# The end of a mixture of experts: the sums of two tables are added on GpSimd before VectorE adds them to the residual

## What is computed

```python
x = x + L0_attn(layernorm(x))
x = x + L0_xattn(layernorm(x), ctx_2048, mask)
x = x + L0_ffn(layernorm(x))        # group attention, then a mixture of experts
x = x + L1_attn(layernorm(x))
x = x + L1_xattn(layernorm(x), ctx_2048, mask)
x = x + L1_ffn(layernorm(x))
```

```python
moe = jnp.einsum('tei,te,eih->th', act, wfull, Wd)
shared = jax.nn.silu(t @ Wsg) * (t @ Wsu) @ Wsd
return resid + (moe + shared).reshape(B, S, H)
```

## Time and profile before

| | |
|---|---|
| median of 3 runs | 2375.61 us (2370.52 to 2378.47) |
| the profiled execution, its own time | 2365.98 us |
| its span, first to last instruction | 2364.2 us |
| mean granted TensorE clock | 0.96 |
| busy: PE, DVE, POOL, ACT | 92%, 55%, 42%, 39% |

### The profile page before, as it was taken

The page is one execution under the profiler, slowest core; times in us unless marked ns, Lnnn a source line. Parts: engine busy times, 40 slices in busy tenths (PEclk is TensorE's granted clock), DMA queues, the critical chain, the costliest instruction groups (busy, mean ns, idle before and its releaser), DMA issues. The chain is left out here.

```text
span 2364.2 us, 40797 instructions
## 1 busy us (share of the span) xinstructions
PE 2163.3 (92%) x14955; PEld 1575.4 (67%) x14955; DVE 1311.1 (55%) x2409; ACT 927.3 (39%) x1667; POOL 987.0 (42%) x852
## 2 busy tenths in 40 slices
PE   7889999798999998879999999697889999989998
PEld 7658877577888887633333333286667777759997
DVE  4563677647787878543333333585862666653333
ACT  1332322335454543236666665214632332322221
POOL 2333565456656564306666665353533110002220
PEclk9899999799999999989999999898999999979999
DMA  3011100221111210466666888620021001001110
GB/s 127 34 50 54 41 28 2 76 67 55 58 54 54 67 45 23 169 231 165 141 144 143 224 219 275 185 81 35 3 77 44 27 27 41 1 27 54 54 53 32
DMA packets 56926, 194.38 MB, mean 82 GB/s; under 512 B 8244, under 2 KB 8500, under 8 KB 49844
## 3 DMA queue, kind: packets, MB, share of 16 engines
q1 hardware_dynamic: 36676, 147.45, 18.0%
q0 software_dynamic: 17280, 38.94, 8.4%
q10 hardware_dynamic: 2784, 5.51, 0.6%
HBM read 158.71 MB, written 33.16 MB: 81 GB/s over the span
## 5 line engine op out<-in xcount | busy, mean ns | idle before, releaser
L2260 PE MATMUL bank<-m_ring,m_bT 128*64 x576 | 266.6, 606 | 3.7 <-ACT m_upper L1988 3.4
L2262 PE MATMUL bank<-m_upper,m_bT 128*64 128x512 f32 x576 | 266.7, 606 | 0.0
L2183 DVE SCALAR_TENSOR_TENSOR m_prod<-bank,m_slot_rows,m_silu 64x256 f32<-64x256 f32 x144 | 69.6, 483 | 276.0 <-ACT m_silu L1934 273.4
L2260 PEld LDWEIGHTS bank<-m_ring,m_bT 128*64 128x64 f32 x576 | 73.9, 138 | 142.6 <-issue 142.6
L1906 POOL DMA_INDIRECT m_sum<-m_yb,m_idx x72 | 102.8, 1428 | 130.3 <-DVE m_yb L2194 111.2
L970 ACT ACTIVATE y_att_p_rows<-bank,y_att_n_top 112x375 f32<-112x375 f32 x128 | 71.6, 572 | 188.6 <-DVE y_att_n_top L1012 188.6
L1988 ACT ACTIVATE m_upper<-m_ring 128x1024 f32 x144 | 143.5, 1046 | 2.5 <-issue 2.4
L2288 PE MATMUL bank<-m_ring,m_aT 128*64 x288 | 135.4, 592 | 0.7 <-DVE m_aT L2200 0.7
L2290 PE MATMUL bank<-m_upper,m_aT 128*64 128x512 f32 x288 | 135.4, 592 | 0.0
L313 PE MATMUL bank<-f_hT_hi,f_w_hi 128*128 128x448 f32 x288 | 113.4, 394 | 13.6 <-POOL f_w_lo L1436 3.2
L2474 POOL TENSOR_TENSOR z_w_lo<-z_raw,z_w_hi 128x1024 fp32r<-128x1024 f32 x21 | 50.6, 2408 | 155.4 <-ACT z_w_hi L2500 155.4
(11 more groups left out here) (477 smaller groups left out, 6208.5 us busy)
## 6 DMA issues: line engine op xcount, KB each, us to landing
m_ring<-in_m_w SPq DMA_DIRECT2D x32, 1536.0 KB, 8.2
f_raw<-in_f_wq SPq DMA_DIRECT2D x64, 256.0 KB, 2.6
z_raw<-in_z_w SPq DMA_DIRECT2D x7, 1536.0 KB, 6.7
f_att_wo_raw<-in_f_wo SPq DMA_DIRECT2D x16, 512.0 KB, 4.1
m_sum<-m_slot_rows SPq DMA_DIRECT2D x4, 2048.0 KB, 18.0
x_c_raw<-in_ctxT SPq DMA_DIRECT2D x8, 752.0 KB, 8.9
y_c_raw<-in_ctxT SPq DMA_DIRECT2D x8, 752.0 KB, 9.7
a_raw<-in_a_wqk SPq DMA_DIRECT2D x8, 256.0 KB, 2.5
```

Of the source, the lines that this page charges most:

```text
L2260: pe.matmul(ps_gu[u % 2][0:HP, :], bT[:, n % 2, k, 0:HP], ring[:, bass.ds(slot + at, D)], start=(k == 0), stop=(k == KC - 1))
L2262: o = pe.matmul(ps_gu[u % 2][HP:P, :], bT[:, n % 2, k, HP:P], upper[:, n % 2, at:at + D], start=(k == 0), stop=(k == KC - 1))
```

## The change

GpSimd gets seven adds behind its last scatter: for each tile it waits for both loads of the pair of tiles and adds `x2` to `y` in place. VectorE loses its seven first adds. It adds `y`, which then holds both tables' sums, to `x`, once per tile, when GpSimd's `first_sum` says that the tile is there. Both shared tiles are now added ahead of all of these.

```diff
@@ GpSimd, behind the last scatter
             scatter(NBLK - 1)
+            for b in range(NT):
+                pool.wait_ge(early_in[b // 2], 16)
+                pool.wait_ge(late_in[b // 2], 16)
+                pool.tensor_tensor(y[:, b, :], y[:, b, :], x2[:, b, :], ALU.add).then_inc(first_sum, 1)
@@ VectorE
-            def add_first(b):
+            def add_sums(b):
                 dve.wait_ge(add_done, b + 1)
-                dve.wait_ge(early_in[b // 2], 16)
-                dve.tensor_tensor(x[:, b, :], x[:, b, :], y[:, b, :], ALU.add).then_inc(first_sum, 1)
-
-            def add_last(b):
-                dve.wait_ge(late_in[b // 2], 16)
                 dve.wait_ge(first_sum, b + 1)
-                dve.tensor_tensor(x[:, b, :], x[:, b, :], x2[:, b, :], ALU.add).then_inc(total_sum, 1)
+                dve.tensor_tensor(x[:, b, :], x[:, b, :], y[:, b, :], ALU.add).then_inc(total_sum, 1)
                 dve.wait_ge(total_sum, b + 1)
                 dve.bn_stats(g.stats[:, b, :], x[:, b, :])
@@ VectorE, the order at the end
             add_shared(5)
-            for b in range(6):
-                add_first(b)
             add_shared(6)
-            add_first(6)
             for b in range(NT):
-                add_last(b)
+                add_sums(b)
```

## The result

The changed kernel takes 2380.74 us in the median of 20 runs (2373.21 to 2388.83), the kernel before 2371.24 us over 20 runs (2364.00 to 2378.47). The ratio is 1.0042, with a 95% interval of 1.0031 to 1.0053. That is 7.4 to 12.6 us slower, where +2.9 us was forecast.

A forecast was written before the change was run, and what follows sets the result against it. VectorE's chain was taken to bound the mixture's end; with GpSimd's adds and turns of 1.69 us it would end at 1535.5 instead of 1532.55, +2.9 us, put on the median 2375.61: 2378.5 us, range 2371 to 2386.

The forecast's parts named there:

- VectorE's chain and not TensorE sets the end of the stage: At the mixture's end, VectorE's seven pairs of add and statistics, ending at 1532.55, were said to hold up the next stage.
- The turns: In the final adds, GpSimd and VectorE, both reading SBUF, were to alternate, five turns of 1.69 us each.
- VectorE's own end: End of VectorE's last statistics in the mixture, forecast at 1535.5 instead of 1532.5, +2.9 us.
- The lower bound: At the mixture's end, without disturbance between the engines, VectorE would finish at 1532.05 to 1532.1, -0.45 us.
- The rival without disturbance: In the final adds, the engines would not hold each other up: -0.45 us, 2375.2 us in all; chance 10%.
- the one in which GpSimd keeps its place until all its adds are done: VectorE's seven pairs would start only after GpSimd's seven adds, at 1530.6: +7.4 us, 2383.0 us; chance 5%.
- Nothing is queued behind these seven adds on GpSimd but the barrier: At the mixture's end, GpSimd's queue was taken to hold only the barrier after its adds, with no further time counted.
- what moves the 1532.55 moves everything behind the barrier by as much: At the mixture's end, any shift of VectorE's end was to shift the barrier and next stage equally.
- it is a mixture that ends 2.9 us later: By the trace, the mixture's end was to come 2.9 us later; chance of this forecast 75%.
- The clock: TensorE's return to full clock, some 3 us after resuming, was to move in step; rival: later, +1.5 us, chance 10%.
- three signs of being wrong: At the mixture's end: GpSimd adds all 1.27 us, VectorE's first add ending after 1530, or x2 loads landing outside 1522 to 1525.

The follow-up runs named there:

- e6: Kernel before, with VectorE adding shared tile 6 ahead of the y adds of tiles 4 and 5: 21.79 us from last scatter to next stage, ratio 0.9989.
- e10: Kernel before, with e6's order and the last adds of tiles 1 to 3 on TensorE: 21.25 us from last scatter to next stage, ratio 0.9997.
- e3: Changed kernel, with VectorE's seven final adds reading a PSUM bank in place of y: 29.58 us from last scatter to next stage, ratio not measured.
- e8: Changed kernel, with a GpSimd drain behind its last scatter and VectorE's final adds reading PSUM: 22.96 us from scatter to next stage, ratio 1.0003.
- e4: Changed kernel without GpSimd's drain at the end of the mixture's block: 25.71 us from last scatter to next stage, ratio 1.0016.
- e2: Kernel before, with GpSimd waiting for VectorE's last add, then setting one unused element: 31.73 us from last scatter to next stage, ratio 1.0043.

## Why the prediction's number held, and where its mechanism failed

What was right: in the kernel before, VectorE's chain and not TensorE sets the end of the stage (in e6 and e10 the chain ends 1.21 and 1.75 us earlier after the scatter, and the next stage begins as much earlier). The turns: 1.69 us forecast for one, 1.67 us measured from one VectorE add to the next (1528.02 to 1529.69 in the trace); first add 1.7 forecast and 1.66 measured, the others 1.0 to 1.1 and 1.03. What GpSimd waits out of VectorE's add is 1.71 - 1.26 = 0.45 of 0.675 us. The Trainium skill, "SBUF — State Buffer", section "Who interferes with whom", states that a VectorE instruction with at most one SBUF input, outside its two-port modes, does not contend with GpSimd. e3 agrees, with 1.256 us for each GpSimd add. The same section of the Trainium skill says that the engine which comes second is fully blocked. That would have been VectorE's whole 0.675 us; the measured 0.45 decides. VectorE's own end: +2.9 forecast, +2.5 measured; 0.3 us of the difference is GpSimd's first add, which began 10.89 us after the last scatter where 11.21 was forecast, and 0.1 us is five turns of 1.67 instead of 1.69. The lower bound was mis-sized: "1532.05 to 1532.1", -0.45 us, took GpSimd's pace for the undisturbed case, while VectorE's slower pairs set it and give 0 (e3, e8). The rival without disturbance, and the one in which GpSimd keeps its place until all its adds are done, are out by the same rows.

The step that failed is "Nothing is queued behind these seven adds on GpSimd but the barrier", and with it "it is a mixture that ends 2.9 us later". GpSimd's drain was queued there, and the term was counted at 0 where it costs 6.0 us (8.6, less the 2.6 by which GpSimd finishes before VectorE). With it fell "what moves the 1532.55 moves everything behind the barrier by as much": in the changed kernel GpSimd's drain sets the end of the stage, not VectorE's chain. That GpSimd's queue ends with its last scatter, as the description of the kernel has it, is not so either. I had read each engine's work after the last scatter and taken GpSimd to be free from 1512.15 on. Its queue was free only from 1520.7; the row of line 1723 stood in the trace of before, among the sequencers' instructions, which count as not busy and appear in none of the views that I read. The sum with it is 2.5 + 6.0 = +8.5 us from scatter to next stage, within the measured 7.4 to 12.6. The median's difference is 9.5; whether the remaining 1.0 is anything can't be told, since in single executions what follows the mixture varies from 829 to 838 us with no change there.

The clock did nearly as forecast. TensorE was idle for 25.3 us instead of 17.5, resumed at 1547.97, and had its full clock again in the window at 1552 (1540 before, after resuming at 1536.76). That is 4.0 us after resuming instead of 3.2, so the rise did not move quite in step, and the transposes took 5.04 us instead of 4.63:

```profile
1551.00:1552.00 1.00, 1.00 (x9) 1.00 (x8) 0.85 (x2) 1.00 (x4) 0.83 (x1) 0.68 0.97 244
1552.00:1553.00 1.00, 1.00 (x10) 0.78 (x8) 0.87 (x2) 1.00 (x4) 1.00 (x2) 1.00 0.80 204
```

As a forecast of the difference, the prediction failed. "Slower by over 0.3%" had 10% of the chances and "the same" 87%, and the measured interval of 0.31 to 0.53% lies wholly in the first. Those chances came from a sum that lacked a term of twice its own size. None of the three signs of being wrong that it names would have shown this: counted from the last scatter, GpSimd's adds, VectorE's first add and the loads behaved as forecast.

That the stated time of 2378.5 us lies so near to the measured 2380.74 is luck. It was put on a median of three runs, 2375.61; over 20 runs the kernel before takes 2371.24, 4.4 us less. The same +2.9 us on that is 2374.1. The range held the time because it was made for the scatter of the runs.

## What to carry to other kernels

Before work is moved to an engine that looks idle, read that engine's queue as well as its busy time: a drain or a barrier that stands behind its last instruction moves along with that instruction, and its price shows as soon as the engine finishes last or nearly so. In this kernel the GpSimd block that has issued 216 indirect transfers closes with 8.6 us of drain (other numbers of them gave 2.7 to 9.2 us), so GpSimd's last instruction should come at least that long before the block's end, or the drain be placed in a wait. And where two engines are to share elementwise work, look for rows in which both run at once, with the same kinds of operands: they gave the length of a turn to 0.02 us.

## What the runs showed of the hardware that was not expected

- A full GpSimd drain (a drain in the queue, or the one that closes the block) ended 8.55 to 8.62 us after GpSimd's last work where 104 or 216 indirect transfers had been issued since the last one, 9.21 us for 112, 5.99 us for 184, 2.67 us for 32 long landed, and 0.07 us where an earlier drain had already covered them, with only adds in between. Up to 112 that is 0.082 to 0.083 us for each transfer; the rule beyond is open.
- The drain in front of the clearing of semaphores took 0.15 us even where no full drain stood between it and 216 indirect transfers, and the next block's closing drain then ended 0.1 us after GpSimd's last work (e4).
- A 1 x 1 memset of 0.09 us on GpSimd cost 8.0 us, by its place in the queue (e2: 9.19 us between VectorE's last statistics and the next stage, against 1.19).
